# An adapter of 20 slots around one ring of banks: the next norm and two pairs of projections move into its last slots, padded weights and first scores into its begin

## The reference, cut to what matters

```python
# layer 0, per batch
query = x @ Wq;  keyt = enc @ Wk;  valt = enc @ Wv            # enc: 73 rows
hs = mha(query, keyt, valt)
q1 = (ca^T @ Wq_ca)[indices]                                  # ca: 4 token rows; 96 channels, repeated to 512
hs1 = mha(q1, x, x)                                           # over the 512 rows of x
hs2 = mha(hs1 @ Wq, ca @ Wk_ca, ca @ Wv_ca)
x = (hs + hs2) @ Wout + b_out + x
# layer 1
x = attention(layer_norm(x, g1, be1), itself, wq1, wk1, wv1, wo1) + x    # self-attention
x = attention(layer_norm(x, g2, be2), context, ...) + x
x = geglu_ff(layer_norm(x, g3, be3)) + x
```

## Time and profile before

| | us |
|---|---|
| median of 3 runs (1038.76 to 1040.11) | 1039.35 |
| the profiled execution | 1038.5 |
| its span, first to last instruction | 1036.7 |
| adapter, its last update of x ends | 157.42 |
| self-attention, first scores | 164.40 |

### The profile page before, as it was taken

The page is one execution under the profiler, slowest core; times in us unless marked ns, Lnnn a source line. Parts: engine busy times, 40 slices in busy tenths (PEclk is TensorE's granted clock), DMA queues, the critical chain, the costliest instruction groups (busy, mean ns, idle before and its releaser), DMA issues.

```text
span 1036.7 us, 17534 instructions
## 1 busy us (share of the span) xinstructions
PE 981.3 (95%) x6376; PEld 707.1 (68%) x6376; DVE 690.3 (67%) x1171; ACT 591.5 (57%) x1332; POOL 380.1 (37%) x493
## 2 busy tenths in 40 slices
PE   7999978999999999999999999999989999999998
PEld 4566666666667656667666667666647589999887
DVE  2767646677773776773676773776753889999563
ACT  2666634766763667763667763667753555455442
POOL 2576623434332344342344341343330024444220
PEclk9999999999999999999999999999999999999999
DMA  6400050000000000000000000000000340000000
GB/s 134 94 2 1 1 147 1 1 1 2 1 1 2 1 1 2 1 1 1 2 1 1 1 1 1 2 1 1 2 1 8 101 110 1 1 1 1 2 26 26
DMA packets 25370, 17.64 MB, mean 17 GB/s; under 512 B 8565, under 2 KB 24101, under 8 KB 25285
## 3 DMA queue, kind: packets, MB, share of 16 engines
q1 hardware_dynamic: 25285, 16.52, 6.6%
HBM read 11.26 MB, written 1.31 MB: 12 GB/s over the span
## 4 chain that ended last, share of the span: by engine, by line
PE 64%; DVE 10%; ACT 5%; issue 4%; POOL 1%; DMA 0%; SPq 0%; DVEq 0%; ACTq 0%; POOLq 0%
PE banks L409 13%; PE banks L396 12%; PE banks L382 11%; PE banks L416 4%; ACT sa_probs L499 3%; PE banks L224 3%; PE banks L227 2%; PE banks L226 2%; PE banks L225 2%; PE banks L1641 2%; PE banks L1933 2%; DVE sa_negmax L571 2%; DVE ca_top L1776 2%; DVE ca_probs L1781 1%; PE banks L232 1%
## 5 line engine op out<-in xcount | busy, mean ns | idle before, releaser
L639 POOL TENSOR_SCALAR sa_probs<-sa_probs,sa_inverse 128x512 f32<-128x512 f32 x320 | 217.7, 696 | 372.4 <-DVE sa_inverse L575 372.3
L499 ACT ACTIVATE sa_probs<-banks,sa_negmax 128x512 f32<-128x512 f32 x320 | 215.8, 685 | 163.5 <-DVE sa_negmax L571 163.4
L571 DVE TENSOR_REDUCE sa_negmax<-banks 128x2 f32<-128x1024 f32 x160 | 188.8, 1219 | 12.4 <-PE banks L382 9.7
L396 PEld LDWEIGHTS banks<-ident,sa_probs 128*128 128x128 f32 x1280 | 145.7, 141 | 55.6 <-issue 27.6
L396 PE MATMUL banks<-ident,sa_probs 128*128 128x128 f32 x1280 | 174.0, 277 | 10.0 <-ACT sa_turned L510 5.8
L580 DVE COPY sa_turned<-banks 128x512 f32<-128x512 f32 x160 | 110.2, 689 | 76.3 <-PE banks L396 76.3
L409 PE MATMUL banks<-sa_turned,sa_v 128*64 128x512 f32 x640 | 155.0, 605 | 0.0
L382 PE MATMUL banks<-sa_k_parts,sa_q_parts 64*128 64x512 f32 x960 | 134.9, 412 | 1.9 <-ACT sa_probs L499 1.9
L510 ACT COPY sa_turned<-banks 128x512 f32<-128x512 f32 x160 | 94.3, 590 | 30.6 <-PE banks L396 28.8
L382 PEld LDWEIGHTS banks<-sa_k_parts,sa_q_parts 64*128 64x128 f32 x960 | 85.2, 187 | 31.2 <-issue 14.4
L409 PEld LDWEIGHTS banks<-sa_turned,sa_v 128*64 128x64 f32 x640 | 38.7, 136 | 74.3 <-issue 73.0
(11 more groups left out here) (218 smaller groups left out, 1724.9 us busy)
## 6 DMA issues: line engine op xcount, KB each, us to landing
w_o<-in_L_xattn_wo SPq DMA_DIRECT2D x2, 800.0 KB, 9.2
out<-x SPq DMA_DIRECT2D x4, 320.0 KB, 2.4
w_q_t<-in_L_xattn_wq_t SPq DMA_DIRECT2D x1, 1120.0 KB, 10.4
fold_values<-ca_turned SPq DMA_DIRECT2D x5, 192.5 KB
x<-in_x SPq DMA_DIRECT2D x1, 960.0 KB, 5.8
fold_values<-ca_probs SPq DMA_DIRECT2D x4, 192.5 KB
w_q_t<-in_L_xattn_wq SPq DMA_DIRECT2D x1, 640.0 KB, 6.6
w_o<-in_L_xattn_wk SPq DMA_DIRECT2D x1, 640.0 KB, 10.0
```

The lines of the kernel that those rows point to most:

```text
L396: last = pe.transpose(b_turn[e][:, q * P:(q + 1) * P], probs[:, j % 2, e, q, k * P:(k + 1) * P], ident[:])
L499: act.activation(probs[:, j % 2, e, q, :], b_scores[u % 2][:, e, :], ACT.Exp, bias=negmax[:, u % RING, e:e + 1], accum_out=total[:, u % RI ...
L571: dve.tensor_reduce(negmax[:, u % RING, :], b_scores[u % 2], AX_X, ALU.max, negate=True).then_inc(s_max.sem, 1)
L639: pool.tensor_scalar(probs[:, j % 2, e, q, :], probs[:, j % 2, e, q, :], inverse[:, u % RING, e:e + 1], 1.0, ALU.mult, ALU.mult).then_inc( ...
```

## The change

At the begin: the seven weights come padded from the host (whole rows of 32 columns per head, one DMA each, no clearing); the context, tokens, wk, wv, wk_ca and wv_ca lie in the memory of `turned`, wq_ca in that of `probs1`. The keys go to banks 4 and 7 and `scores1(0)` stands before them; the wait for the spread token values stands before L1043.

At the end: statistics go to slot 11, normalization to 13, transposes and scaling to 14 (as items of the ring), rounding to 15. New functions project, round and take the rest of the self-attention's pairs 0 and 1 in slots 16 and 17, in banks 0 and 1. q_parts and k_parts are therefore allocated ahead of the adapter, and to make room x_pad has two buffers instead of three, q2 lies in hs1, k_all in the norm's `hat`.

With that, the transposes of x go from k = 0 to k = 1, `pad_x(b + 1)` to k = 0 (b from 1), and the query projection of group 0 from k = 1 to k = 3.

```diff
+NORM_AT = 14
         out += [("probs", u - 1, 0)] if 1 <= u <= units else []
-        if k == 0 and b + 1 < B:
+        if k == 1 and b + 1 < B:
             out += [("x", b + 1, g) for g in range(G)]
-        if k == 1 and b + 1 < B:
-            out += [("queries", b + 1, 0)]
         if k == 2 and 1 <= b <= B:
             out += [("expanded", b - 1, 0)]
+        if s == NORM_AT:
+            out += [("norm", 0, i) for i in range(2)]
         if k == 3 and b < B:
             out += [("folded", b, i) for i in range(2)]
         if k == 3 and b + 1 < B:
-            out += [("queries", b + 1, 1)]
+            out += [("queries", b + 1, g) for g in range(G)]
...
+        b_keys = (banks[4], banks[7])
...
-            sp.wait_ge(s_zero, 5)
-            for tile, name in ((wq_ca, "Wq_ca"), (wk, "Wk"), (wk_ca, "Wk_ca"), (wv_ca, "Wv_ca"), (wv, "Wv")):
-                sp.dma_start(tile[:, :, 0:HD0], by_head(w(name))).then_inc(s_w, 16)
-            sp.wait_ge(s_zero, 7)
-            for h in range(H0):
-                sp.dma_start(wq[to(h), h // HG, :, 0:HD0], by_head(w("Wq")[h * HD0:(h + 1) * HD0, :])).then_inc(s_wq, 16)
+            for tile, name in ((wq_ca, "wq_ca"), (wk, "wk"), (wk_ca, "wk_ca"), (wv_ca, "wv_ca"), (wv, "wv")):
+                sp.dma_start(tile, t["padded_" + name]).then_inc(s_w, 16)
+            sp.dma_start(wq[:], t["padded_wq"]).then_inc(s_wq, 16)
             sp.dma_start(x[:, QT:, :], tiles[:, QT:, :]).then_inc(s_xrest, 16)
-            for h in range(H0):
-                sp.dma_start(wo[to(h), h // HG, :], w("Wout")[h * HD0:(h + 1) * HD0, :]).then_inc(s_wo, 16)
+            sp.dma_start(wo[:], t["padded_wo"]).then_inc(s_wo, 16)
...
             last.then_inc(s_q1p.sem, 1)
+            scores1(0)
             pe.wait_ge(s_ct.sem, s_ct.at(0, 0))
...
-            scores1(0)
             for g in range(G):
                 project_queries(0, g)
+            pe.wait_ge(s_v2t.sem, s_v2t.at(0, G - 1))
...
                 if k == 3 and b + 1 < B:
+                    project_queries(b + 1, 0)
                     project_queries(b + 1, 1)
-                if s == NU + 1:
-                    pe.wait_ge(s_exp1.sem, s_exp1.at(NU - 1, 1))
-                    next_ln.turn(pe, 0, ident, banks[0:2], lambda i: None)
+                if s == NORM_AT:
+                    pair = [("norm", 0, i) for i in range(2)]
+                    next_ln.turn(pe, 0, ident, [ring.bank(banks, item) for item in pair], lambda i: ring.wait_free(pe, pair[i]))
+                    pe.wait_ge(next_ln.s_turned.sem, next_ln.s_turned.at(0, 1))
+                    pe.sem_inc(ring.s_made, 2)
+                if s in (NU, NU + 1):
+                    project_first(s - NU)
...
+            def project_first(j):
+                if j == 0:
+                    next_ln.ready(pe, 0)
+                    pe.wait_ge(s_exp1.sem, s_exp1.at(NU - 1, 1))
+                    pe.wait_ge(s_rest.sem, s_rest.at(len(chunks) - 1, 1))
+                else:
+                    pe.wait_ge(s_qklo.sem, s_qklo.at(0, 1))
+                for i in range(2):
+                    next_ln.project(pe, banks[i], splits[i][1], j * P).then_inc(s_qk.sem, 1)
...
+            def round_first(j):
+                act.wait_ge(s_qk.sem, s_qk.at(j, 0))
+                act.activation(q_parts[:, j, 0, :], banks[0], ACT.Copy, scale=SCALE1).then_inc(s_qkhi.sem, 1)
+                act.wait_ge(s_qk.sem, s_qk.at(j, 1))
+                act.copy(k_parts[:, j, 0, :], banks[1]).then_inc(s_qkhi.sem, 1)
...
-                if s == NU + 1:
+                if s == NORM_AT:
                     act.wait_ge(s_later, 16 * len(later))
-                    next_ln.scale_and_round(act, 0, banks[0:2], lambda eng: None)
+                    next_ln.scale(act, 0, [ring.bank(banks, ("norm", 0, i)) for i in range(2)])
+                    act.wait_ge(next_ln.s_full.sem, next_ln.s_full.at(0, 1))
+                    act.sem_inc(ring.s_act, 2)
+                if s == NORM_AT + 1:
+                    next_ln.round(act, 0, lambda eng: None)
+                if s in (NU, NU + 1):
+                    round_first(s - NU)
...
-                if k == 0 and b + 1 < B:
+                if k == 1 and b + 1 < B:
                     copy_x(b + 1)
+                if k == 0 and 1 <= b and b + 1 < B:
+                    pad_x(b + 1)
                 if k == 3 and b < B:
                     copy_folded(b)
-                if k == 3 and b + 2 < B:
-                    pad_x(b + 2)
-                if s == NU - 2:
+                if s == NORM_AT - 3:
                     dve.wait_ge(s_x.sem, s_x.at(QT - 1, 0))
                     next_ln.statistics(dve, 0)
-                if s == NU - 1:
+                if s == NORM_AT - 1:
+                    dve.wait_ge(s_kd.sem, s_kd.at(B - 1, 0))
                     next_ln.standardize(dve, 0)
-                if s == NU + 1:
+                if s == NORM_AT + 1:
                     next_ln.remainder(dve, 0, lambda eng: None)
+                if s in (NU, NU + 1):
+                    rest_first(s - NU)
```

More of the change, by code:

```diff
@@ L418, in project_out @@
                 return last
[L420 to L424, removed]
+            for s in (s_q, s_k):
+                pe.sem_inc(s.sem, 2)
             scores(0, 0)
@@ L510, in copy_turned @@
                 act.copy(turned[:, u % 2, 1, :], b_turn[1]).then_inc(s_evac_act.sem, 1)
[L512 to L515, removed]
+            for s in (s_qhi, s_khi):
+                act.sem_inc(s.sem, 2)
             exps(0, 0)
@@ L588, in update @@
                     dve.tensor_tensor(xt, b_turn[half][:, 0:2 * D], xt, ALU.add).then_inc(s_x.sem, 1)
[L590 to L593, removed]
+            for s in (s_qlo, s_klo):
+                dve.sem_inc(s.sem, 2)
             maxima(0, 0)
@@ L730, in wait_copied, with adapter @@
         eng.wait_ge(self.copied(item), same.index(item) + 1)
-def adapter(nc, t, x, ident, ctx_t, banks, splits, raws, later, last, next_ln):
+def adapter(nc, t, x, ident, ctx_t, banks, splits, raws, later, last, next_ln, q_parts, k_parts):
     w = lambda n: t["L0_xattn_" + n]
@@ L755, in adapter @@
         own = sb("own", [P, G, H0])
-        context = sb("context", [SK, B, CTX])
-        tokens = sb("tokens", [NCA, B, CTX])
-        x_pad = sb("x_pad", [P, 3, QT, H0, HP])
+        x_pad = sb("x_pad", [P, 2, QT, H0, HP])
         x_t = sb("x_t", [P, 2, G, S])
@@ L930, in products1 @@
                     for j in range(HG):
-                        last = pe.matmul(b_token[j * HP:(j + 1) * HP, g * CTX:(g + 1) * CTX], x_pad[:, b % 3, k, HG * g + j, :],
+                        last = pe.matmul(b_token[j * HP:(j + 1) * HP, g * CTX:(g + 1) * CTX], x_pad[:, b % 2, k, HG * g + j, :],
                                          turned1[:, j, k, :], start=(k == 0), stop=(k == QT - 1))
@@ L1293, in _ @@
             copy_x(0)
+            max1(0)
             dve.wait_ge(s_kp.sem, s_kp.at(0, 0))
-            dve.tensor_copy(k_all[:], b_s1[:, :, 0:B * SK]).then_inc(s_ka.sem, 1)
+            for g in range(G):
+                dve.tensor_copy(k_all[:, g, :], b_keys[g][:, 0:B * SK]).then_inc(s_ka.sem, 1)
             dve.wait_ge(s_w, 16 * N_W)
             for g in range(G):
-                each = b_s1[:, g, B * SK:B * SK + B * NCA].rearrange("p (b t) -> p b t", b=B)
+                each = b_keys[g][:, B * SK:B * SK + B * NCA].rearrange("p (b t) -> p b t", b=B)
                 dve.tensor_tensor(v2_t[:, g, :, :, :], each.unsqueeze(2).broadcast_to([P, B, H0, NCA]),
                                   own[:, g, :].unsqueeze(1).unsqueeze(3).broadcast_to([P, B, H0, NCA]), ALU.mult).then_inc(s_v2t.sem, 1)
-            max1(0)
             dve.wait_ge(s_xrest, 16)
@@ L2065, in build @@
             raws = [Overlaid(main[:].rearrange("p j d -> p (j d)")[:, 0:INNER], rest[:]) for main, rest in ((wq_t, w_k2), (w_o2, w_v2), (w_o1, tail))]
-            adapter(nc, t, x, ident, ctx_t, banks, [(w("wq1"), wa), (w("wk1"), wb), (w("wv1"), wc)], raws, later, last, ln1)
+            q_parts, k_parts = (early.enter_context(nc.sbuf_tensor(n, [P, 2, 2, S], F32R)) for n in ("sa_q_parts", "sa_k_parts"))
+            adapter(nc, t, x, ident, ctx_t, banks, [(w("wq1"), wa), (w("wk1"), wb), (w("wv1"), wc)], raws, later, last, ln1, q_parts, k_parts)
             block = ctx.enter_context(nc.Block())
-            x_ready = selfattn(nc, block, x, ident, ln1, ln2, wa, wb, wc, w_o1, bias["bo1"], banks)
+            x_ready = selfattn(nc, block, x, ident, ln1, ln2, wa, wb, wc, w_o1, bias["bo1"], banks, q_parts, k_parts)
         with ExitStack() as folding:
@@ L2088 @@
     arrays["in_expand"] = (np.arange(CTX)[:, None] == repeated[None, :]).astype(np.float32)
+    for name in ("Wq_ca", "Wk", "Wk_ca", "Wv_ca", "Wv"):
+        matrix = arrays.pop("in_L0_xattn_" + name)
+        padded = np.zeros((matrix.shape[0], H0, HP), np.float32)
+        padded[:, :, 0:HD0] = matrix.reshape(-1, H0, HD0)
+        arrays["in_padded_" + name.lower()] = padded
```

(6 more changed lines are left out.)

71 lines of the change are left out of this document (35 added, 36 removed).

## The result

The changed kernel takes 1046.95 us (median of 5 executions, 1045.55 to 1050.79) against 1038.76 of the kernel before on the same chip: ratio 1.0082, 95% interval 1.0067 to 1.0096, slower by 8 us where 3 were forecast, and outside the range. Its profiled execution is the fastest of the five, 1045.55 with a span of 1043.5, which is 7.05 and 6.8 above the execution profiled before. The longer executions have a lower mean granted clock (0.982 in the one of 1050.79, 0.990 in the profiled one).

The account below looks back on a forecast made before the run. TensorE, busy 95% of the span, bounds the kernel, so a later adapter end moves everything behind it. Begin −1.0, middle +3.8 and end +0.3 give +3.1 on the median 1039.35: 1042.5 us, range 1036.5 to 1045.5.

Parts of the forecast that it names:

- half pace behind the hand-over: First self-attention scores and values run slowly after TensorE idles at the adapter's end: 0.5 us taken, bounds 0 to 1.
- The middle: Slots 1 to 12: query projections moved to k = 3 cost 5.6 us, 1.8 come back; +3.8, bounds +0.3 and +5.2.
- The two gaps: Slot 14: TensorE idle before the last transpose and before the norm's second set of transposes, 1.8 us each.
- the give-back's sum: Time regained in slots with k of 0 to 2: 1.3 us in slots 8 to 10, 0.4 in slots 4 to 6.
- The begin: Adapter's start: padded weight loads give 0.5 us, scores ahead of the keys 0.5 more; together −1.0.
- the clock in slots 14 and 15: Slots 14 and 15: no clock loss in the sum; slot 15, full of TensorE work, takes nothing back of +5.0.
- The sum: Whole kernel: −1.0 + 3.8 + 0.3 = +3.1 us, giving 1042.5; chance 0.42.
- The rival that had the clock fall: Slots 14 and 15: idle gaps lower TensorE's clock, costing 1.3 to 1.7 us more, 1044.2 us; chance 0.15.
- Against it: short work lies between: Slot 14: argument against a clock fall, since the expansion and transposes stand between the two 1.8 us idle times.
- The hand-over's bound: Adapter's end to first self-attention scores: 5.48 us of projections go, 0 to 1 returns as slow pace; −5.0 taken.
- The moved work evens out: Middle: slots with k of 0 to 2 give back what k = 3 takes, cost 0; 1038.7 us, chance 0.26.
- TensorE's work alone: Adapter: only TensorE's work sets its time, so middle and slot 14 cost nothing; −6 us, 1033.4, chance 0.17.

Follow-up runs that it names:

- e3: The changed kernel with its end put back as before, begin and middle kept; ratio 1.0052 to the kernel before, median 1043.94 us.
- e2: The kernel before with only the middle of the change (x transposes, query projections, two x_pad buffers); ratio 1.0043 to the kernel before.
- e7: The changed kernel with six unread matmuls, three in each of two gaps of slot 14, no wait removed; ratio 1.0046 to the kernel before.
- e4: The changed kernel with nine unread matmuls, three and six in two gaps of slot 14, no wait removed; ratio 1.0048 to the kernel before.
- e11: The kernel before with ScalarE's part of the first norm behind the last expansion and VectorE's remainder behind update(12); ratio 0.9952 to the kernel before.
- e6: The changed kernel with the norm's statistics in slot 10 and normalization in slot 11, its transposes still in slot 14; ratio 1.0055 to the kernel before.
- e13: The kernel before with query projection between the fold's halves, first norm behind the last expansion, and the change's begin; ratio 0.9958 to the kernel before.
- e5: The changed kernel with the norm's statistics in slot 10, normalization in 11, transposes in 13, rounding in 14; ratio 1.0034 to the kernel before.
- e9: e5 with the first query projection between the two halves of the folding; ratio 1.0030 to the kernel before.

## Why the prediction was wrong

Its steps against the traces:

| | forecast | changed kernel |
|---|---|---|
| scores1 of slot 1 | 24.4 | 25.00 |
| slot 12, later by | 2.8 | 2.56 |
| slot 15, later by | 7.8 | 7.99 |
| from slot 15 to the next transposes, longer by | 0 | 3.08 |
| adapter's last update, later by | 8.1 | 10.59 |
| first scores behind it | 2 | 1.83 |
| first scores, later by | 2.6 | 5.44 |
| half pace behind the hand-over | 0.5 | 1.4 |
| span, longer by | 3.1 | 6.8 |

- **The middle and slot 14: right in mechanism.** Slots 3, 7 and 11 each hold two projections in 3.67 us behind the fold's wait. The two gaps have the place and the cause that were named, 1.99 at full pace and 1.62. That the give-back's sum fits (1.8 us where 1.7 were taken, for slots 4 to 6 and 8 to 10) is partly luck: slots 8 to 10 gave 0.74 and not 1.3, slots 4 to 6 1.08 and not 0.4. One reading was wrong: update(7) stands ahead of the 0.51 us of idle time, so it had to come the full 2.55 later and not 2.0; the 1.8 for the last transpose follows from the 2.55.
- **The begin: less than forecast.** The padded weights let the token queries start at 7.93 and not 8.55, and slot 0's token scores wait 0.99 us (0.9 forecast). At slot 12 it is worth 0.59 (e3 against e2) to 0.92 (the changed kernel against e2), with 1.0 forecast.
- **The failed step is the clock in slots 14 and 15.** The sum took it as unchanged, a cost of nothing, where slot 15 took 3.08 us more; of the 3.7 us by which the trace exceeds the sum, 3.1 are these. The rival that had the clock fall, at a chance of 0.15, named the mechanism, but priced it by the stretches of the earlier trace rows, 2.6 to 3.4 us of work, at 1.3 to 1.7. The half pace lasted 6.5 us of work in slot 15 and cost 3.1 (3.2 against e7). "Against it: short work lies between" was no argument: TensorE worked 3.69 of 5.90 us there and the clock fell all the same. This cost is shown: e4 and e7 keep 1.00 in slot 15, and their intervals lie wholly below the changed kernel's.
- **The hand-over's bound was too narrow.** 5.48 went, as forecast, but 1.6 of them had been half pace (3.89 in e11), and behind the hand-over 1.4 came back and not 0.5. The bound of 1 was below what the prediction's own row gives: 3.4 us at half pace are 1.7 of loss.
- **The rivals.** "The moved work evens out" falls with e2; "TensorE's work alone" falls with e7's 1.99 us of waiting. What the prediction cites on transposes from the Trainium skill ("TensorE: Matmul & The Clock Gate", section "Part 4: PE-mode transpose") gave the right sign, since 2.1 of the 3.69 us between 126.00 and 131.90 are transposes; but no run here separates transposes from idle time.
- **The median.** The trace says +7.05, the medians +8.2: four of the five executions are longer than the profiled one, those of 1046.95 and more with a clock of 0.987 or less.

Open is what makes the clock fall. Gaps alone don't decide it: e7 keeps 1.00 with its wait of 1.99 us. Nor does the work alone. Slots 12 and 13 and the gap of 0.74 stand in the kernel before and in e3 as well, 2.6 us earlier and 0.3 later, and there the clock stayed at 1.00 with nothing filled; in the changed kernel, in e6 and in e13 it fell behind that gap. And e5 and e9 have the same rows of TensorE in slot 14: 1.2 us of the norm's transposes, the scores, a gap of 1.57. First e5, then e9:

```profile
124.34 0.85 PE L909 MATMUL banks<-ident,ad_probs 96*128 96x96 f32 x8 [1.57 <-ACTq L1210]
125.03 1.28 PE L1007 MATMUL banks<-ad_folded,ad_turned 128*128 128x160 f32 x8
```
```profile
122.11 1.51 PE L913 MATMUL banks<-ident,ad_probs 96*128 96x96 f32 x8 [1.57 <-ACTq L1215]
123.41 2.39 PE L1013 MATMUL banks<-ad_folded,ad_turned 128*128 128x160 f32 x8
```

e5's slot 14 takes 7.35 us and e9's 10.51. So the same gap can cost nothing more or 3.2 us more, and each kernel has one trace here. That the fall in slot 15 merely follows the one in slot 14 is unlikely, since e9 and e13 have the first and not the second. What the fillings changed, the idle time or the share of ordinary matmuls in it, no run separates.

## What to carry to other kernels

Price a new gap on TensorE as the gap, and give half pace behind it a chance and a price of its own (3.1 us here, more than the trace before had shown); work moved out of the end of a stage may hand its slow pace to what comes next. The slow stretch ahead of a stall cost nothing here, and the one behind it all of its length. A difference of one or two microseconds in one trace says little where the clock falls at other places from kernel to kernel: set it against the times of several executions. Before moving matmuls into a stage to shorten its hand-over, read which engine's queue holds its last small step: here two conditions changed in two queues gave 5 us, where the whole rearrangement cost 8.

## What was not expected of the hardware

VectorE's normalization, the same four instructions L153, took four different times, and they go with GpSimd's. First in the kernel before, in the self-attention and as VectorE's work of slot 15; then in the changed kernel (VectorE's work of slot 13), then in e6 (of slot 11). Of the five busy times in a row, VectorE's is the third and GpSimd's the fifth:

```profile
228.91:230.08 1.17, 1.17 (x12) 0.69 (x12) 1.17 (x6) 0.20 (x1) 0.17 (x1) 1.00 0.00 0
133.41:135.96 2.55, 2.55 (x21) 2.40 (x21) 2.55 (x6) 0.88 (x2) 1.90 (x2) 1.00 1.04 252
```
```profile
122.19:125.42 3.23, 3.23 (x14) 3.23 (x15) 3.23 (x6) 0.86 (x2) 2.91 (x4) 0.52 0.02 5
```
```profile
104.19:108.13 3.94, 3.94 (x11) 1.48 (x11) 3.93 (x5) 1.00 (x2) 3.67 (x4) 1.00 0.00 0
```

With 0.17 us of GpSimd beside it 1.17, with 1.90 2.55, with 2.91 3.23, with 3.67 3.94. The Trainium skill ("SBUF — State Buffer", section "Who interferes with whom") says that a tensor_scalar of VectorE can enter a mode that needs a pair of ports shared with GpSimd, and that whoever issues first then holds the pair for its whole instruction while the other waits. The four rows agree in direction: above 1.17, VectorE took 1.38, 2.06 and 2.77 us more beside 1.90, 2.91 and 3.67 us of GpSimd's work. But no row shows the mode, and no run here takes GpSimd's work away. It is also where slot 14's forecast fell short: priced at 2.55, the normalization took 3.23, and from the start of slot 14 to its last transpose it was 8.04 us (119.66 to 127.70) against 5.71 before (117.10 to 122.81), 2.3 more and not 1.8. An instruction of VectorE that is moved beside GpSimd's should be priced by a row with GpSimd as busy.
